# A start-up reordered in a recommendation tower: new order of transfers, and ScalarE copies e with its dimensions turned

## The reference, cut to what matters

```python
e = jnp.stack([tbl_0[ids[:, 0]], ..., tbl_38[ids[:, 38]]], axis=1)      # (2048, 39, 16)
x, outs = e, []
for W in (W0, W1):                                 # (128, 39*39), (128, 128*39)
    inter = (x[:, :, None, :] * e[:, None, :, :]).reshape(B, last * F, D)
    x = jnp.einsum('bid,hi->bhd', inter, W)        # (2048, 128, 16)
    outs.append(x.sum(axis=-1))
z = jnp.concatenate(outs, axis=-1)
h = jnp.concatenate([z, dense_ctx], axis=1)        # dense_ctx: (2048, 16)
h = jnp.maximum(h @ W_top1 + b_top1, 0.0)
h = jnp.maximum(h @ W_top2 + b_top2, 0.0)
y = h @ W_top3
```

## Time and profile before

| what | value |
|---|---|
| three runs | 786.94, 788.52, 789.17 us; median 788.52 |
| profiled execution | 789.04 us, of which the span on the core is 787.2 us |
| PE busy | 696.7 us (88%) |
| DVE busy | 676.3 us (86%) |
| POOL busy | 532.5 us (68%) |
| ACT busy | 420.1 us (53%) |
| granted TensorE clock, mean | 0.985 |

### The profile page before, as it was taken

How to read it: one execution, slowest core, us unless ns; L and a number is a source line. 1 busy time by engine, 2 the same in 40 slices (tenths; PEclk the granted TensorE clock), 3 DMA queues, 4 the chain that set the end, 5 groups by cost and what they waited for, 6 DMA issues and landing times.

```text
span 787.2 us, 17029 instructions
## 1 busy us (share of the span) xinstructions
PE 696.7 (88%) x6210; PEld 594.9 (76%) x6210; DVE 676.3 (86%) x865; ACT 420.1 (53%) x769; POOL 532.5 (68%) x406
## 2 busy tenths in 40 slices
PE   0222477899999999999999999999999999999997
PEld 0221355687888888888888888888888888888887
DVE  5661699999999999999999999999999999988810
ACT  0001255656665666656565666565666656576641
POOL 6777788888878787878888888888887873000000
PEclk9997699999999999999999999999999999999999
DMA  4269869697876868686969676787878695754000
GB/s 106 66 133 271 152 161 182 164 163 170 171 160 151 144 172 144 169 157 163 182 160 169 152 169 134 182 139 184 135 182 142 162 167 154 160 151 132 14 7 1
DMA packets 171030, 115.67 MB, mean 147 GB/s; under 512 B 135043, under 2 KB 146906, under 8 KB 170563
## 3 DMA queue, kind: packets, MB, share of 16 engines
q1 hardware_dynamic: 156310, 110.49, 61.0%
q0 software_dynamic: 12800, 3.30, 6.2%
q10 hardware_dynamic: 1837, 0.78, 0.4%
HBM read 104.08 MB, written 15.53 MB: 152 GB/s over the span
## 4 chain that ended last, share of the span: by engine, by line
PE 76%; DVE 10%; DMA 4%; POOL 3%; issue 3%; SPq 3%; ACT 0%; DVEq 0%; ACTq 0%
PE z_ps L423 18%; PE x_ps L383 12%; PE x_ps L387 11%; PE x_ps L384 11%; PE g_ps L413 8%; DVE product_lo L671 5%; DVE products L663 4%; PE x1T_ps L444 4%; PE aux_ps L372 4%; POOL e_rows L359 3%; PE x1T_ps L402 3%; PE x1T_ps L436 2%; DMA id_spread<-id_scratch 2%; PE x1T_ps L434 2%; SPq L263 1%
## 5 line engine op out<-in xcount | busy, mean ns | idle before, releaser
L359 POOL DMA_INDIRECT e_rows<-in_tbl_dram,ids_sb x400 | 532.1, 1330 | 123.5 <-issue 119.5
L513 ACT CAST product_hi<-products 117x1024 fp32r<-117x1024 f32 (+1 forms) x256 | 242.7, 948 | 129.9 <-DVE products L663 126.9
L671 DVE TENSOR_TENSOR product_lo<-products,product_hi 117x1024 fp32r<-117x1024 f32 (+1 forms) x256 | 278.0, 1086 | 24.3 <-ACT product_hi L513 24.0
L663 DVE TENSOR_TENSOR products<-bases 117x1024 f32<-117x1024 f32 (+1 forms) x256 | 277.8, 1085 | 2.3 <-DMA bases<-eT_scratch 1.8
L383 PE MATMUL x_ps<-product_hi,w_hi 117*128 117x512 f32 x448 | 198.7, 444 | 10.5 <-ACT product_hi L513 5.9
L384 PE MATMUL x_ps<-product_hi,w_lo 117*128 117x512 f32 x448 | 178.3, 398 | 0.0
L423 PE MATMUL z_ps<-G,w1T 128*128 128x128 f32 x1248 | 178.1, 280 | 0.0
L423 PEld LDWEIGHTS z_ps<-G,w1T 128*128 128x128 f32 x1248 | 165.0, 191 | 17.3 <-issue 0.5
L387 PE MATMUL x_ps<-product_lo,w_hi 117*128 117x512 f32 x448 | 148.4, 401 | 29.5 <-DVE product_lo L671 29.4
L387 PEld LDWEIGHTS x_ps<-product_lo,w_hi 117*128 117x128 f32 x448 | 84.3, 190 | 54.6 <-DVE product_lo L671 34.7
L383 PEld LDWEIGHTS x_ps<-product_hi,w_hi 117*128 117x128 f32 x448 | 85.7, 191 | 24.9 <-issue 9.2
(11 more groups left out here) (54 smaller groups left out, 358.7 us busy)
## 6 DMA issues: line engine op xcount, KB each, us to landing
bases<-eT_scratch SPq DMA_DIRECT2D x155, 468.0 KB
e_diag<-e_scratch SPq DMA_DIRECT2D x512, 10.0 KB
id_spread<-id_scratch SPq DMA_DIRECT2D x16, 437.5 KB
e_rows<-in_tbl_dram,ids_sb POOLq DMA_INDIRECT x400
e_scratch<-e_d SPq DMA_DIRECT2D x16, 320.0 KB
eT_scratch<-e_rows SPq DMA_DIRECT2D x16, 312.0 KB
eT_scratch<-eT_scratch SPq DMA_DIRECT2D x16, 312.0 KB, 3.2
w1T<-in_L_rec_W_dram SPq DMA_DIRECT2D x1, 2496.0 KB, 16.4
```

The source lines that it names most:

```text
L359: nc.gpsimd.indirect_dma_start(out=e_rows[t % E_SLOTS][:, f * D:(f + 1) * D], out_offset=None, in_=tables[f], in_offset=bass.IndirectOffse ...
L513: nc.scalar.copy(product_hi[:, first:first + count, :], products[:, first:first + count, :]).then_inc(hi_ready, 1)
L663: nc.vector.tensor_tensor(products[:, first:first + count, :], bases[u % 2][:, b:b + count, cols], bases[u % 2][:, a:a + 1, cols].to_broad ...
L671: nc.vector.tensor_tensor(product_lo[:, first:first + count, :], products[:, first:first + count, :], product_hi[:, first:first + count, : ...
```

## The change

SP loads 7 of the 14 tables and ACT the other 7, ahead of its W0 loads. SP stores the turned ids and spreads tiles 0 and 1 before the three dense weight loads, and `spread_ids(2)` comes right after those, ahead of `store_eT(0)`. The first bases are loaded half by SP and half by ACT. w1T is loaded in the loop after `spread(0)`, the network's weights after `spread(3)`. `copy_e` and the rounding of `split_dense` go from DVE to ACT: `copy_e(0)` behind the W0 loads, `copy_e(t+1)` at the end of ACT's step g = 4t. The split of the tables ends with a subtraction that writes the third bf16 part directly, where before a subtraction and a cast did it (five DVE instructions become four).

```diff
+        def load_base_part(queue, t, first, count, ready):   # was SP's own; body the same
...
-            for n, f in enumerate(LOOKED):
+            for n, f in enumerate(LOOKED[:NS // 2]):
                 sp.dma_start(tab_f[...], tables[f]...).then_inc(tab_loaded, 16)
-            sp.wait_ge(zeroed, 1)
-            for n in range(3):
-                sp.dma_start(wt1_dense_f[...], w_top1[...]).then_inc(wt1_dense_loaded, 16)
             sp.wait_ge(id_turned_ready, 2)
...
             spread_ids(0)
             spread_ids(1)
+            sp.wait_ge(zeroed, 1)
+            for n in range(3):
+                sp.dma_start(wt1_dense_f[...], w_top1[...]).then_inc(wt1_dense_loaded, 16)
+            spread_ids(2)
             store_eT(0)
             store_e(0)
             double_eT(0)
             sp.wait_ge(eT_doubled, 16)
-            for c in range(2):
-                load_base_part(0, c * (HB // 2), HB // 2, first_ready[c])
-            sp.dma_start(w1T[:, :, :], w1).then_inc(w1_loaded, 16)
-            ... five loads, mlp_loaded
-            spread_ids(2)
+            load_base_part(sp, 0, 0, HB // 2, first_ready[0])
             for g in range(CHUNKS):
...
                 spread(g)
+                if g == 0:
+                    sp.dma_start(w1T[:, :, :], w1).then_inc(w1_loaded, 16)
+                if g == 3:
+                    ... the five loads, mlp_loaded
...
-            pe.wait_ge(tab_split, 2 * PARTS - 1)
+            pe.wait_ge(tab_split, 2 * PARTS - 2)
...
         def _(act):
+            for n, f in list(enumerate(LOOKED))[NS // 2:]:
+                act.dma_start(tab_f[...], tables[f]...).then_inc(tab_loaded, 16)
             act.wait_ge(zeroed, 1)
...          (34 loads of W0)
+            copy_e(0)
+            act.wait_ge(eT_doubled, 16)
+            load_base_part(act, 0, HB // 2, HB // 2, first_ready[1])
             round_products(0, 0)
...
+                if c == 1 and 0 <= t - 2 < TILES - 2:
+                    round_dense(t - 2)
                 if g < CHUNKS:
                     round_products(g, 2)
...
                 if g + 1 < CHUNKS:
                     round_products(g + 1, 1)
+                if c == 0 and t + 1 < TILES:
+                    copy_e(t + 1)
+                if g == CHUNKS - 1:
+                    round_dense(TILES - 2)
+                if g == CHUNKS + CPT:
+                    round_dense(TILES - 1)
...
         def _(dve):      # copy_e(t) and the rounding in split_dense(t) are gone
-            for part in range(PARTS):
+            for part in range(PARTS - 1):
                 after(dve, tab_split, 2 * part)
                 nc.vector.tensor_copy(tab[:, part, :], tab_f).then_inc(tab_split, 1)
-                if part < PARTS - 1:
-                    dve.wait_ge(tab_split, 2 * part + 1)
-                    nc.vector.tensor_tensor(tab_f, tab_f, tab[:, part, :], ALU.subtract).then_inc(tab_split, 1)
+                dve.wait_ge(tab_split, 2 * part + 1)
+                rest = tab[:, PARTS - 1, :] if part == PARTS - 2 else tab_f
+                nc.vector.tensor_tensor(rest, tab_f, tab[:, part, :], ALU.subtract).then_inc(tab_split, 1)
```

More of the change, by code:

```diff
@@ L235, in cin_tower @@
         y_stored = sem("y_stored")
+        def load_base_part(queue, t, first, count, ready):
+            at = first % HB * D
+            for a, starts in enumerate(BASES):
+                step = starts[1] - starts[0]
+                part = eT_scratch[t, starts[0]:starts[0] + 1, first:first + count, :].rearrange("f b d -> f (b d)")
+                blocks = bass.AP(part.tensor, part.offset, [[TB * D, F], [step * TB * D, BLOCKS], [1, count * D]])
+                queue.dma_start(bases[first // HB][:, a, at:at + count * D], blocks).then_inc(ready, 16)
         block = ctx.enter_context(nc.Block())
@@ L254, in double_eT @@
                 sp.dma_start(eT_scratch[t, F:2 * F, :, :], eT_scratch[t, 0:F, :, :]).then_inc(eT_doubled, 16)
[L256 to L263, removed]
             def load_bases(u):
@@ L270, in load_bases @@
                 after(sp, product_ready, (u - 1) * 2 * NG)
-                load_base_part(t, h * HB, HB, bases_ready[h])
+                load_base_part(sp, t, h * HB, HB, bases_ready[h])
             def spread(g):
@@ L312, in _ @@
             spread_ids(1)
+            sp.wait_ge(zeroed, 1)
+            for n in range(3):
+                sp.dma_start(wt1_dense_f[n * GAP:n * GAP + D, :], w_top1[2 * H:2 * H + D, :]).then_inc(wt1_dense_loaded, 16)
+            spread_ids(2)
             store_eT(0)
@@ L333, in _ @@
                 spread(g)
+                if g == 0:
+                    sp.dma_start(w1T[:, :, :], w1).then_inc(w1_loaded, 16)
+                if g == 3:
+                    sp.dma_start(wt1_cin[:, :, :], w_top1[0:2 * H, :].rearrange("(k p) n -> p k n", p=128)).then_inc(mlp_loaded, 16)
+                    sp.dma_start(wt2[:, :, :], w_top2.rearrange("(k p) n -> p k n", p=128)).then_inc(mlp_loaded, 16)
+                    sp.dma_start(wt3[:, :], w_top3).then_inc(mlp_loaded, 16)
+                    sp.dma_start(bias1[:, :], b_top1).then_inc(mlp_loaded, 16)
+                    sp.dma_start(bias2[:, :], b_top2).then_inc(mlp_loaded, 16)
                 if c == 0 and t + 1 < TILES:
@@ L555, in copy_y, with copy_e, round_dense @@
                 nc.scalar.copy(y, mlp_ps[0:1, 2, :]).then_inc(y_ready, 1)
+            def copy_e(t):
+                act.wait_ge(gathered[t % E_SLOTS], (t // E_SLOTS + 1) * 16 * len(GATHERED))
+                act.wait_ge(looked_up, (t + 1) * sum(map(len, SETS)))
+                after(act, e_stored, 16 * t)
+                nc.scalar.copy(e_d[:, :, 0:F], e_rows[t % E_SLOTS][:, :].rearrange("b (f d) -> b d f", d=D)).then_inc(e_d_ready, 1)
+            def round_dense(t):
+                act.wait_ge(dense_loaded, (t + 1) * 16 * 3 * GAP // D)
+                after(act, h1_in_ps, M1 * t)
+                nc.scalar.copy(dense_parts[:, :], dense_now[:, :]).then_inc(dense_hi_ready, 1)
+            for n, f in list(enumerate(LOOKED))[NS // 2:]:
+                act.dma_start(tab_f[:, K_FIRST[n] * D:K_FIRST[n + 1] * D], tables[f].rearrange("(p k) d -> p (k d)", k=K_OF[n])).then_inc(tab_loaded, 16)
             act.wait_ge(zeroed, 1)
@@ L602, in _ @@
         def _(dve):
[L603 to L607, removed]
             def make_one_hot(t, n):
@@ L646, in split_dense @@
             def split_dense(t):
-                dve.wait_ge(dense_loaded, (t + 1) * 16 * 3 * GAP // D)
-                after(dve, h1_in_ps, M1 * t)
-                nc.vector.tensor_copy(dense_parts[:, :], dense_now[:, :]).then_inc(dense_hi_ready, 1)
                 dve.wait_ge(dense_hi_ready, t + 1)
@@ L729, in _ @@
                                     wt1_dense[2 * GAP:3 * GAP, :].bitcast(f32), ALU.subtract).then_inc(wt1_dense_split, 1)
-            copy_e(0)
             make_k_mask(1)
@@ L748, in _ @@
                     pick_rows(t + 1, 3)
-                if c == 0 and t + 1 < TILES:
-                    copy_e(t + 1)
                 if c == 1 and t >= 2:
```

6 lines of the change are left out of this document (removed).

## The result

The changed kernel takes 780.16 us (median of four runs, 779.41 to 780.98) against 788.85 us on the same chip: a ratio of 0.9891, 95% interval [0.9864, 0.9917]. It is faster, by 8.6 us of span (787.2 to 778.6) where 15.5 were forecast. 780.16 lies in the range 765 to 781, but not in the 768 to 776 of the likeliest case; it lies in the 776 to 781 of the rival "the queues cost more".

The account below looks back on a forecast made before the run. TensorE's chain (76%) bounds the span, its work untouched; DVE sets the pace for about two early tiles after its stall. Terms -15.5 + 1.5 - 1.5 = -15.5 us took 789.04 to 773.5, as median 773.0; range 765 to 781.

Parts of the forecast that it names:

- the likeliest case: Whole kernel: the forecast from the summed terms, 768 to 776 us, chance 0.55.
- the queues cost more: Rival: first bases at 64, w1T until 82, network's loads 6 us; 776 to 781 us, chance 0.20.
- The stall: DVE's 22.5 us wait for tile 2's `id_spread` goes; third group's products start at 63.9 instead of 85.56.
- Tables, ids, W0: Loads and look-ups at the start, beside tile 0's gathers: counted 0 us, bounds -1 to +2.
- The first bases: Tile 0's first half of bases there at 60: 57 if issuing was the limit, 64 if moving was.
- ACT's wait at `copy_e(1)`: End of ACT's step 0: ACT held some 4 us by tile 1's gathers; cost 0 to 4, taken as 1.
- Tile 1's way: Store, doubling, spread and bases of tile 1: first product at 104.5 (101 to 107), 15.5 us earlier.
- The network's loads: Five issues on SP after `spread(3)` delay chunk 6 and tile 2's way: +1.5 us, bounds 0 to 6.
- DVE without `copy_e`: Tiles 2 and 3, where DVE sets the pace: saves up to 2.3 us, counted -1.5.
- The floor by gathers: Tile 2's later gathers and ACT's place for `copy_e(2)` allow no more than 16 to 18 us gain there.
- The steady part: Later tiles: ACT's `copy_e`, 0.7 to 0.85 us, fits the wait before the copy of x1; 0 us.
- The slower rival: Gathers become the bound at 44.3 us a tile, so the end comes near 798 us; chance 0.06.

Follow-up runs that it names:

- e7: The changed kernel with all 14 tables loaded by SP, as before the change; 779.38 us, ratio 0.9897.
- e11: e10 with all 14 tables loaded by SP, as in e7; 775.35 us, ratio 0.9853.
- e5: The kernel before, with only `spread_ids(2)` moved ahead of `store_eT(0)`; 785.45 us, ratio 0.996.
- e6: The changed kernel with both halves of the first bases loaded by SP, as before the change; 786.08 us, ratio 0.9962.
- e9: e5 with the copy of e on ACT for every tile, transfers of the start in the old order; 781.98 us, ratio 0.9926.
- e3: The changed kernel with w1T loaded after chunk 2's spread instead of chunk 0's; 783.33 us, ratio 0.992.
- e12: e11 with w1T issued by ACT behind its W0 loads; 775.53 us, ratio 0.9854.
- e4: The changed kernel with the five network loads after chunk 6's spread instead of chunk 3's; 778.21 us, ratio 0.9871.
- e10: The changed kernel with only the five network loads moved ahead of `spread_ids(2)` on SP; 774.81 us, ratio 0.9842.
- e8: The changed kernel with w1T and the five network loads moved ahead of `spread_ids(2)` on SP; 775.74 us, ratio 0.9854.
- e1: The changed kernel with `copy_e(2)` to `copy_e(15)` back on DVE at their old place; 782.01 us, ratio 0.9894.

## Why the prediction came out as it did

**The stall.** Right. The 22.5 us are gone; the one-hot of tile 2 starts at 66.67 with no wait, and the third group's products follow at once, 3 us after the forecast 63.9, because the first were late.

**Tables, ids, W0: 0.** Within its bounds of -1 to +2: tile 0 is stored at 40.46, 0.83 us later than before, and e7 and e11 move the tables without a measurable effect on the time.

**The first bases: 60.** The upper bound, 64, was the right one: 63.15. The lower, 57, had no ground: the five loads of the first half stand first on SP in both kernels, so a second queue can't bring their issue forward. 1.2 us are a later start of the loads (49.32 against 48.10); the rest goes with sharing. Where one queue issues both halves, the first is used 11.1 to 11.6 us after the first issue (before, e5, e6, e9); where two do, after 12.9 to 15.5 (all the others). The Trainium skill ("DMA: Bandwidth & Descriptors", section "Issuing engines are not separate DMA queues") has it that all issues run on the same 16 DMA engines and several issuing engines save only the issue time, which is usually small beside the transfer itself. The first half agrees with that. The saved issue time, 6.4 us on SP against 13.8 us until the first half was used, was not small here: e6, which lacks it, is slower by 0.71% in the ratio, about 5.6 us, with intervals apart. The forecast did not price what leaves SP's queue earlier.

**ACT's wait at `copy_e(1)`: cost 1 (0 to 4).** The place was right and ACT waited 5.1 us, where 4 were expected. But the reason was off: the gathers were issued by 72.05, before the expected 74.3, the last of them in 0.99 us beside a DVE that was busy from 64 to 72 without a gap; and they landed 8.3 us later, not 1.4. To DVE it cost 2.89 us at 83.08 and 0.36 more. e3 shows w1T's part: without it ACT waits 0.4 us, and 3.4 of the 8.3 us go.

**Tile 1's way: 104.5 (101 to 107).** 106.98, with 2.60 us of wait for bases, as described. w1T until 82: it landed at 82.7. The way from the store of tile 1 began at 80.37, where 104.5 less the 25 us of the text is 79.5, and took 26.6 us: that is the 2.5 us too much. From t0 to t1 it took 43.83 us. Without waits DVE needs 37.68 (e12), so 6.15 us are lost there, the "about 6" of the text: 2.60 at the bases and 3.25 at the rounding that ACT delivers late. PE's granted clock was 0.51 from 80 to 88, its lower level of 1.2 GHz, as in the earlier trace rows, after PE had stood idle 8.36 us up to 82.16; the waits named leave 0.3 of the 6.15 us for it.

**The network's loads: +1.5 (0 to 6).** This step was the furthest off by size: 4.7 us, by e4 against after. The prediction named who waits behind them, but priced issues only and took the slack of SP as cover. SP's slack at the store of tile 2 is 2.0 us (e4) against 3.1 us of issues, and most of the loss comes behind that store, which starts at the same time in both: the next store's issue, 6.77 us against 1.98, and the doubling, 132.11 against 127.06.

**DVE without `copy_e`: -1.5.** Right for DVE, but hardly to be seen in after. Where nothing waits, tile 1 to tile 2 takes 39.72 us (e12) against 40.89, and tile 2 to tile 3 40.29 against 41.31: 2.2 us together, the upper end. In after the waits for transfers cover nearly all of it: tile 1 to tile 4 takes 4.46 us more than before, and 4.7 of it are the network's loads, so some 0.2 us of relief are left. The floor by gathers (16 to 18 us) was not reached.

**The steady part: 0.** Right (542.75 against 542.76 us), though ACT's copy takes 1.30 us and not 0.7 to 0.85; the cover held.

**The sum.** -13.05 at tile 1, +4.41 from tile 1 to tile 2, +0.05 from there to tile 4: -8.6. Forecast were -15.5, +1.5 and -1.5. Of the 6.9 us between -15.5 and -8.6, 2.5 are tile 1's way, 3.2 the network's loads and 1.3 the relief that DVE could not use. The likeliest case took a middle or low value at two steps that each ended near the bound that the full queue gave: 63.15 of 57 to 64, 4.7 of 0 to 6. The rival "the queues cost more" had nearly these terms (64, w1T until 82, 6), and that it was inside the range is why the range held; the sum of the likeliest case did not. The slower rival fell: ACT waited for gathers at two tiles only.

**Not settled.** How much of the cost of the network's loads is their issue on SP and how much their bytes was not tried apart; e4 speaks for the bytes. The gathers' total time, 532.1 us before and 509.5 after, was expected to profit from the copy on ACT, by the Trainium skill ("SBUF — State Buffer", section "Who interferes with whom"). For a DVE instruction with two SBUF inputs that section has it only of GpSimd instructions that read SBUF, a condition that the prediction left out. The runs don't show a profit: the total is 500.0 in e5, where DVE copies, and 531.2 in e10, where ACT does. And no place was found where w1T is free: it put tile 0 off by 6 to 7 us (e8, e12), or the way from tile 0 to tile 1 was 4 to 6 us over DVE's 37.7 (e10, after), or `id_spread` came late (7.75 us of wait in e3).

## What to carry to other kernels

When a stall goes, price what its time had been hiding: here it hid the loads of weights, and each load that is moved out of the stall needs a place where nothing urgent is queued behind it on the issuing engine or in the DMA engines. If the engines have no idle time over a stretch, take the bound that moving gives for every step in it, not the middle. A load needed late was best put into a gap ahead of the critical transfers where it is small (the network's loads, 1,028 KB: 0.49% between the ratios of e10 and after, about 3.9 us); the large one (w1T, 2,496 KB) cost 4 to 8 us at each place that was tried.

## What was not expected of the hardware

- The same store of e (320 KB, one instruction) took SP 12.40 us to issue in e5 and 11.65 in e1, but 1.98 in e4. What still moves ahead of it shows as a long issue and not as a wait: after against e4, which differ only in the place of the network's loads, have 6.77 and 1.98.
- In after the indirect gathers of tile 1 had landed 8.3 us after POOL was done with them, with the DMA engines 0.96 to 1.04 busy (64 to 80), those of tile 0 1.4 us after, with 0.35 (32 to 40) and 0.67 (40 to 48).
- ScalarE's copy of 128x624 f32 with dimensions turned takes 1.25 to 1.30 us, VectorE's 0.69 to 0.83.
- w1T (2,496 KB) landed 20.4 us after its issue behind the bases (after) and 12.5 us after its issue at 32.76 (e12).
